# Packing the odd chunk's gate and up rows into one product, moving attention ticks and down products at quarter ends, and shifting weight splits, start tiles and the last steps

## The chip, the cores and the metric

The kernel runs on one core of a Trainium2 chip. The metric is the time of one execution in microseconds of device time; the number to beat is the median of three runs of the kernel before. The engines are named as the profile names them: PE (TensorE matmuls), PEld (its weight loads), DVE (VectorE), ACT (ScalarE), POOL (GpSimd) and SP (SyncE, which only issues DMAs here).

## The reference

`x` is 16 x 64 tokens of width 256, so 1024 tokens. Two layers follow each other, each an attention to a context of 64 keys per batch row and then a feed-forward part, each added to `x` with a gate `tanh(g)`.

```python
x = x + tanh(g_xattn[0]) * L0_xattn(layernorm(x), ctx, ctx)      # 32 query heads, 8 key heads, 64 keys
x = x + tanh(g_ffn[0])   * L0_ffn(layernorm(x), ...)             # hidden size 704, weights int32
x = x + tanh(g_xattn[1]) * L1_xattn(layernorm(x), ctx, ctx, Wc, bc)   # 16 heads in 4 groups, then Wc and bc
x = x + tanh(g_ffn[1])   * L1_ffn(layernorm(x), ...)             # 32 experts of 96, the best 8 per token

# L0_ffn: W = (wq - 128) * scale[:, None]
gate = silu(einsum('bsd,hd->bsh', x, Wgate)); up = einsum('bsd,hd->bsh', x, Wup)
return einsum('bsh,dh->bsd', gate * up, Wdown)

# L1_ffn: masked_w holds a softmax over the 8 largest router logits of a token, zero for the other experts
g = einsum('th,eih->tei', x, w_gate_proj); u = einsum('th,eih->tei', x, w_up_proj)
h = silu(g) * u * masked_w[:, :, None]
return einsum('tei,ehi->th', h, w_down_proj)
```

## The kernel before

**Tiles and passes.** The 1024 tokens are eight tiles of 128 (TT). The hidden rows of both feed-forward parts are cut into chunks of 128: the dense one has 704 rows, which is five full chunks and one of 64 padded with zeros to 128 (F0 = 6), the experts have 24 (MC). A loop of 72 steps `s` runs over passes: passes 0 to 3 are the dense part, each a quarter of the tokens (256) and six steps; passes 4 and 5 are the experts, each half of the tokens (512) and 24 steps. All experts are computed for all tokens, and the routing weights mask them.

**Precision.** A large product is three matmuls into one bank: high part by high part, low part of the data by high part of the weights, and high by low (`product`; L1298, L1299, L1300). So weights and hidden values are split into a high part (ACT: `wh`, `hh`) and the low remainder (`wl`, `hl`). The remainder of the dense weights is made by DVE (`w_low`, L948) from the integers, that of the experts by POOL (L558). SP loads weights into three buffers (`load`, L469) and waits with the fourth load until the first buffer has been split. Behind that load stand in SP's program the DMAs that move key blocks (`move_keys`, L461).

**One step.** PE computes gate(s) into bank 0, up(s) into bank 1, and down(s-1) into banks 2 to 5. Between them ACT makes `tanh` of the gate, DVE makes `(1 + tanh) * gate` (`gate`, L999) and its product with the up bank (`multiply`, L1009 in the dense part, L1012 for the experts); for the experts DVE then multiplies by the routing weights, which PE has spread over the partitions in bank 7 (`weigh`, L1018). ACT rounds the result to `hh`, and DVE takes the rest `hl` (`split_h`, L1023). So down(s) can only run a step later.

**Attention beside it.** An attention block is a tick: scores of the next block (L1156), values of an earlier one (L1195) and transposes of the present one's probabilities (L1176), with maximum, difference, reciprocal and normalising on DVE (L891, L899, L909, L916), the exponential on ACT (L705). The first sixteen ticks of layer 0 run alone, ahead of step 0. All further ones are put into steps by the table `BESIDE`: for a step, a list of ticks at place 0 (between gate and up) and a list at place 1 (behind down). `tick(k, n)` of the same place stands on each engine in that engine's own step, so the table orders all queues at once.

**Ends of quarters.** When a quarter is through, ACT scales the result (`take_out`), PE transposes it back into bank 2 (`back_quarter`) in step 7, 13, 19 or 25 (`BACK_AT`), and DVE adds it to `x` (`add_quarter`, L1034). The first down product of the next quarter writes the same bank and waits for that.

```python
if s in BACK_AT:
    back_quarter(BACK_AT[s])
for k, n in beside(s, 0):
    tick(k, n)
up(s)
if s:
    down(s - 1)
for k, n in beside(s, 1):
    tick(k, n)
if s + 1 in START:
    q_transposes(A[1], START[s + 1] * HT)
```

**Start of layer 1.** Its attention runs in two halves, which `START` opens at steps 14 and 27: layer norm of the first tiles, `q_split` on POOL (L537, L540), `q_transposes` (L1134), `scores`.

**End.** After step 71 the last down product runs, ACT and DVE scale the two banks, PE transposes eight blocks (L1368), DVE adds them to `x` tile by tile (L1040), SP stores.

## Time and profile before

| | us |
|---|---|
| three runs | 422.61, 424.72, 425.23 |
| median | 424.72 |
| the profiled execution's own time | 426.17 |
| its span in the profile | 424.3 |
| mean granted TensorE clock, as a share of full speed | 0.988 |

The profiled execution has 1.87 us outside its span and lies 1.45 us above the median. Sixteen ticks alone fill the time up to about 50 us, the dense quarters with attention beside them the next 130 or so, and from then on the experts' steps, the second half of layer 1's attention beside the first of them. "PEclk" is the clock that was granted to TensorE, as a share of full speed: 1.0 is 2.4 GHz, 0.5 is 1.2 GHz. A wait is put down to the instruction whose end released it.

### The profile page before, as it was taken

The page shows a single profiled execution, that of the slowest core. Times are in us where ns is not written, and L with a number is a line of the kernel's source. Part 1 is how long each engine was busy: PE and PEld are TensorE (multiplying, and loading weights), DVE is VectorE, ACT ScalarE, POOL GpSimd, SP SyncE. Part 2 cuts the span into 40 slices and gives each one's busy share as a digit, 9 for nine tenths or more (in the row PEclk, how much of TensorE's full clock was granted, in tenths as well). Part 3 has the DMA queues.
Part 4 walks back from the last instruction along what each step waited for, and adds up shares of the span by engine and source line. Part 5 has one row for each costly group of instructions (what it writes and reads, how often), then busy time and mean ns, then how long its engine had stood idle before and what let it go on. Part 6 is the DMA issues. An engine that isn't in the chain of part 4 may idle for free.

```text
span 424.3 us, 6897 instructions
## 1 busy us (share of the span) xinstructions
PE 387.4 (91%) x2258; PEld 336.1 (79%) x2258; DVE 302.2 (71%) x612; ACT 220.7 (52%) x441; POOL 174.2 (41%) x201
## 2 busy tenths in 40 slices
PE   4888989989977987969999999999999999999994
PEld 3777879979967977958788778888787888888883
DVE  5699888777755777677777676665877666666664
ACT  3577866556455653545655544445444444444431
POOL 5954332512435113247534343554353444353510
PEclk9999899989998999999999999999999999999999
DMA  5911211110000110032221211223223243323101
GB/s 132 274 45 49 50 28 31 50 44 0 2 0 10 21 20 3 4 110 76 75 76 54 72 50 63 76 74 108 70 85 100 86 133 104 103 84 111 39 0 49
DMA packets 20818, 27.16 MB, mean 64 GB/s; under 512 B 10928, under 2 KB 13616, under 8 KB 20784
## 3 DMA queue, kind: packets, MB, share of 16 engines
q1 hardware_dynamic: 20784, 26.73, 21.7%
q8 instruction: 18, 0.29, 0.3%
q14 instruction: 16, 0.13, 0.1%
HBM read 24.36 MB, written 1.05 MB: 60 GB/s over the span
## 4 chain that ended last, share of the span: by engine, by line
PE 48%; DVE 4%; ACT 1%; SPq 1%; issue 1%; DMA 1%; POOL 0%; DVEq 0%; ACTq 0%
PE bank L1298 14%; PE bank L1300 14%; PE bank L1299 14%; PE bank L1195 1%; SPq L461 1%; PE bank L1218 1%; PE bank L1176 1%; PE bank L1156 1%; PE bank L1385 1%; DMA kbd<-khl 1%; DVE t_t L1012 0%; DVE h_t L1018 0%; DVE t_t L999 0%; DVE hl L1023 0%; POOL wl L558 0%
## 5 line engine op out<-in xcount | busy, mean ns | idle before, releaser
L558 POOL TENSOR_TENSOR wl<-wraw,wh 128x768 fp32r<-128x768 f32 x48 | 88.8, 1850 | 105.1 <-DVE hl L1023 105.1
L1298 PE MATMUL bank<-xh,wh 128*128 128x512 f32 (+1 forms) x288 | 108.5, 377 | 2.8 <-DVE t_t L999 2.7
L1300 PE MATMUL bank<-xh,wl 128*128 128x512 f32 (+1 forms) x288 | 102.5, 356 | 0.0
L1299 PE MATMUL bank<-xl,wh 128*128 128x512 f32 (+1 forms) x288 | 102.3, 355 | 0.0
L656 ACT ACTIVATE hh<-h_t 128x512 fp32r<-128x512 f32 (+1 forms) x72 | 40.3, 560 | 98.7 <-DVE h_t L1018 81.2
L1298 PEld LDWEIGHTS bank<-xh,wh 128*128 128x128 f32 x288 | 54.9, 191 | 10.7 <-DVE t_t L999 2.2
L1023 DVE TENSOR_TENSOR hl<-h_t,hh 128x512 fp32r<-128x512 f32 (+1 forms) x72 | 43.4, 603 | 24.8 <-ACT hh L656 24.7
L1300 PEld LDWEIGHTS bank<-xh,wl 128*128 128x128 f32 x288 | 54.6, 190 | 7.9
L1299 PEld LDWEIGHTS bank<-xl,wh 128*128 128x128 f32 x288 | 55.0, 191 | 6.7
L999 DVE SCALAR_TENSOR_TENSOR t_t<-s_t,bank 128x512 f32<-128x512 f32 (+1 forms) x72 | 42.9, 595 | 23.6 <-ACT s_t L791 23.0
L1298 PE MATMUL bank<-hh,wh 128*128 128x512 f32 (+1 forms) x144 | 51.6, 359 | 8.7 <-DVE x L1034 5.3
L1195 PEld LDWEIGHTS bank<-vbd,pts 128*128 128x128 f32 x384 | 50.0, 194 | 2.7
L1300 PE MATMUL bank<-hh,wl 128*128 128x512 f32 (+1 forms) x144 | 51.2, 356 | 0.0
L1299 PE MATMUL bank<-hl,wh 128*128 128x512 f32 (+1 forms) x144 | 51.2, 355 | 0.0
L891 DVE TENSOR_REDUCE mx<-bank 128x8 f32<-128x512 f32 x48 | 33.0, 687 | 24.2 <-PE bank L1156 24.1
L1195 PE MATMUL bank<-vbd,pts 128*128 128x72 f32 x384 | 49.2, 272 | 0.0
L656 ACT ACTIVATE pts<-bank 128x256 f32<-128x256 f32 x96 | 31.5, 381 | 30.5 <-PE bank L1176 30.3
L791 ACT ACTIVATE s_t<-bank 128x512 f32<-128x512 f32 x48 | 28.6, 596 | 26.6 <-PE bank L1300 26.4
L705 ACT ACTIVATE pt<-dt_ 128x512 f32<-128x512 f32 x48 | 30.3, 632 | 20.5 <-DVE dt_ L899 20.4
L656 ACT ACTIVATE wh<-wraw 128x768 fp32r<-128x768 f32 x48 | 40.2, 838 | 0.0
L1156 PE MATMUL bank<-kbd,qt 128*128 128x512 f32 (+1 forms) x128 | 36.0, 386 | 3.1 <-DVE dt_ L899 1.5
L1298 PEld LDWEIGHTS bank<-hh,wh 128*128 128x128 f32 x144 | 27.1, 188 | 14.1 <-issue 5.8
(106 smaller groups left out, 571.9 us busy)
## 6 DMA issues: line engine op xcount, KB each, us to landing
wraw<-w SPq DMA_DIRECT2D x54, 384.0 KB, 3.1
kbd<-khl SPq DMA_DIRECT2D x80, 8.0 KB
out<-x SPq DMA_DIRECT2D x8, 128.0 KB, 2.5
kbd<-khl SPq DMA_DIRECT2D x40, 16.0 KB
x<-x_in SPq DMA_DIRECT2D x2, 256.0 KB, 3.7
ctx_v<-ctx_in SPq DMA_DIRECT2D x2, 256.0 KB, 6.2
x<-x_in SPq DMA_DIRECT2D x1, 512.0 KB, 5.6
ot<-sel_in SPq DMA_DIRECT2D x1, 512.0 KB, 5.2
```

What stands on the lines that cost most here:

```text
L558: ops.tensor_tensor(wl[:, slot, :], wraw[:, i % WRAW, :], wh[:, slot, :].bitcast(F32), ALU.subtract).then_inc(F.w_split, 1)
L656: return nc.scalar.activation(dst, src, ACT.Copy, scale=scale)
L705: nc.scalar.activation(pt[:, n % 2, :], dt_[:, n % 2, :], ACT.Exp, scale=a.scale).then_inc(a.p_ready, 1)
L791: nc.scalar.activation(s_t[:, s % 2, 0:w], bank[GB][:, 0:w], ACT.Tanh, scale=sgh[:, c:c + 1] if s < MOE0 else 0.5).then_inc(F.s_ready, 1)
L891: return chains[a.layer].mark(ops.reduce_max(mx[:, n % 2, :], s, AX.X))
L999: ops.scalar_tensor_tensor(t_t[:, k, 0:w], s_t[:, k, 0:w], 1.0, bank[GB][:, 0:w], ALU.add, ALU.mult).then_inc(F.sg_done, 1)
L1023: ops.tensor_tensor(hl[:, k, 0:w], h_t[:, k, 0:w], hh[:, k, 0:w].bitcast(F32), ALU.subtract).then_inc(F.h_split, 1)
L1156: done = nc.tensor.matmul(bank[a.s_bank(n)][:, i * a.ns:(i + 1) * a.ns], qt[:, t % 2, b2, 2 * gp:2 * gp + 2, :].rearrange("p g s -> p (g s)"),
L1195: done = nc.tensor.matmul(bank[a.v_bank(q)][:, gp * P:gp * P + VW], pts[:, n % 2, j, :], a.values_of(pair, q), start=(pair == 0), stop=(pa ...
L1298: nc.tensor.matmul(o, wh[:, slot, w_sl], rh, start=first, stop=False, skip_group_check=reopened)
L1299: nc.tensor.matmul(o, wh[:, slot, w_sl], rl, start=False, stop=False, skip_group_check=reopened)
L1300: return nc.tensor.matmul(o, wl[:, slot, w_sl], rh, start=False, stop=stop, skip_group_check=reopened)
```

## The change

It has seven parts.

1. **One product for the last chunk.** The sixth dense chunk has 64 real rows. The host now puts its up rows into the 64 padded rows of the gate weights, so that one product of 128 rows gives both: gate in partitions 0 to 63 of bank 1, up in 64 to 127. In steps 5, 11, 17 and 23 (`halved`) PE computes no gate(s); the joint product stands where up(s) stands. `tanh` and `(1 + tanh) * gate` read bank 1, `multiply` reads its upper half.
2. **Quarter ends.** In steps 7, 13 and 19 the ticks of place 0 go to place 1, and in all steps of `BACK_AT` down(s-1) comes behind the ticks of place 1.
3. **Splitting the dense weights.** ACT first writes the integers as floats (`w_float`, into the new tile `wf`), then copies these to `wh`; POOL instead of DVE makes `wl`. A buffer is free for the next load once `wf` is made.
4. **Start of layer 1.** Layer norm of the second start tile, its `q_split`, the q copies and `q_transposes` come one step earlier; on POOL the second `q_split` now stands ahead of the next `power`.
5. **Experts.** `weigh` is applied to `(1 + tanh) * gate` ahead of the up product's arrival, `multiply` makes the result; the matmul that spreads the routing weights stands ahead of up(s).
6. **The end.** The sums up to step 69 are taken out at step 70 (unscaled); in step 71 eight fp32 matmuls with the identity put them, tokens as rows, into banks 2 and 3 (`open_rows`). The down products of steps 70 and 71 then take the hidden values as the stationary side and add rows on top (`down_rows`), and two DVE instructions scale and add `x`, followed by the stores (`add_pair`). The scaled take-out, the eight transposes and the four additions behind step 71 are gone.
7. `x_high` of layer 1 waits for the gate product's count, since the halved steps have no up count.

```diff
-          12: (((0, 31),), ((0, 32),)), 13: (((0, 33),), ((0, 34),)), 14: (((1, 0),), ((0, 35),)),
+          12: (((0, 31),), ((0, 32),)), 13: ((), ((0, 33), (0, 34))), 14: (((1, 0),), ((0, 35),)),
...
+def halved(s):
+
+    return s < MOE0 and s % F0 == F0 - 1
...
+def gate_bank(s):
+    return UB if halved(s) else GB
...
-                    sp.wait_ge(F.w_split, i - WRAW + 1)
+                    sp.wait_ge(F.wf_ready if i - WRAW < F0 else F.w_split, i - WRAW + 1)
...
-                slot = (i - F0) % SLOTS
-                ops.tensor_tensor(wl[:, slot, :], wraw[:, i % WRAW, :], wh[:, slot, :].bitcast(F32), ALU.subtract
+                slot = (i if i < F0 else i - F0) % SLOTS
+                src = wf[:, i % 2, :] if i < F0 else wraw[:, i % WRAW, :]
+                ops.tensor_tensor(wl[:, slot, :], src, wh[:, slot, :].bitcast(F32), ALU.subtract
...
+                if s + 2 in START:
+                    q_split(A[1], START[s + 2] * HT + 1)
                 if s + 1 in START:
                     t = START[s + 1] * HT
                     power(A[1], t + 2, t + 4)
-                    q_split(A[1], t + 1)
...
+            def w_float(i):
+                act.wait_ge(F.w_loaded[i % WRAW], 16 * (i // WRAW + 1))
+                if i >= 2:
+                    act.wait_ge(F.w_split, i - 1)
+                nc.scalar.activation(wf[:, i % 2, :], wrawi[:, i % WRAW, :], ACT.Copy, bias=-ZERO_POINT
+                                     ).then_inc(F.wf_ready, 1)
...
                 if i < F0:
-                    nc.scalar.activation(wh[:, i, :], wrawi[:, i % WRAW, :], ACT.Copy, bias=-ZERO_POINT
-                                         ).then_inc(F.wh_ready, 1)
+                    act.wait_ge(F.wf_ready, i + 1)
+                    copy(wh[:, i, :], wf[:, i % 2, :]).then_inc(F.wh_ready, 1)
...
+                if 2 <= n < 2 + 3 * F0 and (n - 2) % 3 == 0:
+                    w_float((n - 2) // 3)
...
-                if s + 1 in START:
-                    layer_norm(A[1], START[s + 1] * HT + 1)
-                    q_copy(A[1], START[s + 1] * HT)
-            take_out(2 + QP - 1)
+                if s + 2 in START:
+                    layer_norm(A[1], START[s + 2] * HT + 1)
+                    q_copy(A[1], START[s + 2] * HT)
...
+            def weigh(s):
+                k = s % 2
+                dve.wait_ge(F.sg_done, s + 1)
+                dve.wait_ge(R.spread_done, (pass_of(s) - QP) * QUADS + quad(s) + 1)
+                ops.tensor_tensor(t_t[:, k, :], bank[MASK][:], t_t[:, k, :], ALU.mult).then_inc(F.weighed, 1)
...
+                if halved(s):
+                    ops.scalar_tensor_tensor(h_t[0:HALF, k, 0:w], bank[UB][HALF:P, 0:w], suh[0:HALF, c:c + 1],
+                                             t_t[0:HALF, k, 0:w], ALU.mult, ALU.mult).then_inc(F.m_done, 1)
...
+                    dve.wait_ge(F.weighed, s - MOE0 + 1)
+                    ops.tensor_tensor(h_t[:, k, :], bank[UB][:], t_t[:, k, :], ALU.mult).then_inc(F.m_done, 1)
...
+                dve.wait_ge(F.pair_done, i + 1)
+                ops.scalar_tensor_tensor(x[:, t0:t0 + 2, :], bank[BACK[1][2 * i]][:].rearrange("p (t d) -> p t d", d=DM),
+                                         tg[:, 3:4], x[:, t0:t0 + 2, :], ALU.mult, ALU.add).then_inc(F.x_done, 2)
...
-                multiply(s)
                 if s >= MOE0:
                     weigh(s)
+                multiply(s)
...
             split_h(STEPS - 1)
-            take_out(QP + 1)
-            for t in range(HT):
-                add_tile(QP + 1, t)
+            for i in range(HT // 2):
+                add_pair(i)
...
             def gate(s):
+                if halved(s):
+                    return
...
+                projection(s, GB, 0).then_inc(F.g_done, 1)
+
+            def projection(s, b, at):
+                tok = tokens(pass_of(s))
                 for h in range(KC):
-                    done = product(bank[GB][:, 0:width(s)], slice(h * P, (h + 1) * P), slot_of(s), xh[:, h, tok],
+                    done = product(bank[b][:, 0:width(s)], slice(at + h * P, at + (h + 1) * P), slot_of(s), xh[:, h, tok],
...
+                if halved(s):
+                    if s < F0:
+                        pe.wait_ge(F.w_split, s + 1)
+                    projection(s, UB, 0).then_inc(F.g_done, 1)
+                else:
+                    projection(s, UB, DM).then_inc(F.u_done, 1)
...
+            def open_rows():
+
+                pe.wait_ge(F.ot_act, KC * QP + 2)
+                pe.wait_ge(F.ot_dve, 2)
+                pe.wait_ge(F.x_done, TT + HT)
+                for t in range(HT):
+                    for h in range(KC):
+                        nc.tensor.matmul(bank[BACK[1][t]][:, t % 2 * DM + h * P:t % 2 * DM + (h + 1) * P],
+                                         ot[:, h, t * P:(t + 1) * P], ident[:], start=(t % 2 == 0 and h == 0), stop=False,
+                                         skip_group_check=True)
+
+            def down_row(s, t, hs, ws):
+                return nc.tensor.matmul(bank[BACK[1][t]][:, t % 2 * DM:(t % 2 + 1) * DM], hs[:, s % 2, t * P:(t + 1) * P],
+                                        ws[:, slot_of(s), 2 * DM:3 * DM], start=False, stop=last(s), skip_group_check=True)
+
+            def down_rows(s):
+
+                pe.wait_ge(F.hh_ready, s + 1)
+                for t in range(HT):
+                    down_row(s, t, hh, wh)
+                    down_row(s, t, hh, wl)
+                pe.wait_ge(F.h_split, s + 1)
+                for t in range(HT):
+                    done = down_row(s, t, hl, wh)
+                    if last(s) and t % 2:
+                        done.then_inc(F.pair_done, 1)
+                if not last(s):
+                    done.then_inc(F.dn_done, 1)
...
+                if s == STEPS - 1:
+                    open_rows()
                 for k, n in beside(s, 0):
                     tick(k, n)
+                if s > MOE0 and (s - MOE0) % CPQ == 0:
+                    spread(s)
                 up(s)
-                if s:
-                    down(s - 1)
+                if s == MOE0:
+                    spread(s)
+                if s and s not in BACK_AT:
+                    down_rows(s - 1) if by_rows(s - 1) else down(s - 1)
                 for k, n in beside(s, 1):
                     tick(k, n)
-                if s + 1 in START:
-                    q_transposes(A[1], START[s + 1] * HT)
-            down(STEPS - 1)
-            for t in range(HT):
-                back_tile(QP + 1, t)
+                if s in BACK_AT:
+                    down(s - 1)
+                if s + 2 in START:
+                    q_transposes(A[1], START[s + 2] * HT)
+            down_rows(STEPS - 1)
...
-    down0 = np.pad(A(L0_ffn_wq_down).T, ((0, pad), (0, 0)))
+    down0 = np.pad(A(L0_ffn_wq_down).T, ((0, pad), (0, 0)), constant_values=int(ZERO_POINT))
+    gate0[HIDDEN:] = up0[HIDDEN - HALF:HIDDEN]
```

The next rows are PE's in step 7, the end of the first quarter: bank0 is gate, bank1 up, bank2 holds the quarter's transposed result and the next quarter's down product, bank3 and bank4 scores, bank5 transposed probabilities, bank6 values. Before:

```order
L1300 MATMUL bank0<-xh,wl 128x256
L1358 MATMUL bank2<-ident,ot 128x128 x4
L1233 MATMUL bank7<-ident,xm 128x128 x2
L1156 MATMUL bank4<-kbd,qt 128x512 x2
L1195 MATMUL bank6<-vbd0,pts 128x72 x4
L1176 MATMUL bank5<-ident,pt 128x128 x4
L1298 MATMUL bank1<-xh,wh 128x256
...
L1298 MATMUL bank2<-hh,wh 128x256
```

And after:

```order
L1405 MATMUL bank2<-ident,ot 128x128 x4
L1342 MATMUL bank1<-xh,wh 128x256
...
L1277 MATMUL bank7<-ident,xm 128x128 x2
L1200 MATMUL bank4<-kbd,qt 128x512 x2
L1239 MATMUL bank6<-vbd0,pts 128x72 x4
L1220 MATMUL bank5<-ident,pt 128x128 x4
L1342 MATMUL bank2<-hh,wh 128x256
```

The tick's rows (L1233 to L1176 before) have moved from ahead of the up product to between it and the down product that follows the transposed result in bank 2.

DVE in the same step: `x` is the quarter's addition, `t_t` and `h_t` are gate and multiply of step 7, the rows from `mx` to `gws` are the tick's. Before:

```order
L891 TENSOR_REDUCE mx<-bank4 128x8
L909 RECIPROCAL rc<-bank6 128x16
L916 TENSOR_TENSOR yt<-bank6,rc 64x2x8x8 x2
L942 TENSOR_TENSOR xl<-bank7,xh 128x2x128
L899 TENSOR_TENSOR dt_<-bank4,mx 128x512
L973 CAST gws<-gw 128x2x32
L975 TENSOR_TENSOR gws<-gw,gws 128x2x32
L1034 TENSOR_TENSOR x<-bank2,x 128x512
L999 SCALAR_TENSOR_TENSOR t_t<-s_t,bank0 128x256
L1009 SCALAR_TENSOR_TENSOR h_t<-bank1,suh,t_t 128x256
```

And after:

```order
L1070 TENSOR_TENSOR x<-bank2,x 128x512
L1027 SCALAR_TENSOR_TENSOR t_t<-s_t,bank0 128x256
L1047 SCALAR_TENSOR_TENSOR h_t<-bank1,suh,t_t 128x256
L927 TENSOR_REDUCE mx<-bank4 128x8
L945 RECIPROCAL rc<-bank6 128x16
```

The addition, gate and multiply now stand ahead of the whole tick.

POOL around step 12, where layer 1 starts: `qs` are the two halves of a split query tile, `x<-x,yt` is a residual addition of layer 0, `ve`, `rstd`, `nmr` belong to layer norms. Before:

```order
L540 TENSOR_TENSOR qs<-xn,qs 128x4x64
L575 TENSOR_TENSOR x<-x,yt 128x256
L523 TENSOR_SCALAR ve2<-mv2 128x1
L525 TENSOR_TENSOR rstd2<-ve2,neghalf 128x1
L527 TENSOR_SCALAR nmr2<-mv2,rstd2 128x1
L507 TENSOR_SCALAR ve<-mv 128x2
L510 TENSOR_TENSOR rstd<-ve,neghalf 128x2
L514 TENSOR_SCALAR nmr<-mv,rstd 128x1 x2
L537 TENSOR_TENSOR qs<-xn,one 128x4x64
L540 TENSOR_TENSOR qs<-xn,qs 128x4x64
```

And after:

```order
L565 TENSOR_TENSOR qs<-xn,qs 128x4x64
L562 TENSOR_TENSOR qs<-xn,one 128x4x64
L565 TENSOR_TENSOR qs<-xn,qs 128x4x64
L601 TENSOR_TENSOR x<-x,yt 128x256
L548 TENSOR_SCALAR ve2<-mv2 128x1
```

The second start tile's split no longer stands behind the residual addition and the two groups of layer-norm rows.

## Rows read from the trace of the kernel before

**Rows 1.** PE's waits: us in total, times, longest.

```profile
PE bank L1298 <- DVE x L1034: 5.3, 3, 2.0
```

**Rows 2.** Windows: length; PE, PEld, DVE, ACT, POOL busy; PEclk, DMA share, GB/s.

```profile
21.00:50.00 29.00, 25.92 (x181) 23.22 (x180) 26.96 (x57) 22.75 (x54) 12.81 (x22) 0.94 0.14 38
93.50:94.80 1.30, 1.30 (x8) 1.30 (x7) 0.97 (x5) 0.21 (x1) 0.00 (x0) 0.50 0.00 0
322.00:413.00 91.00, 91.00 (x404) 74.98 (x403) 61.20 (x91) 40.44 (x62) 37.09 (x21) 1.00 0.28 84
```

**Rows 3.** Groups by form, weight splits: count | busy, mean ns | idle before, releaser.

```profile
L948 DVE SCALAR_TENSOR_TENSOR wl<-wraw,wh 128x768 fp32r<-128x768 int32 x6 | 6.3, 1058 | 0.1
L734 ACT ACTIVATE wh<-wraw 128x768 fp32r<-128x768 int32 x6 | 5.0, 836 | 0.0
L558 POOL TENSOR_TENSOR wl<-wraw,wh 128x768 fp32r<-128x768 f32 x48 | 88.8, 1850 | 105.1 <-DVE hl L1023 105.1
```

**Rows 4.** SP's queue, its wait for the first split: us, times, longest.

```profile
SPq L469 <- DVE wl L948: 9.1, 1, 9.1
```

**Rows 5.** Timeline of the opening, POOL and SP's queue: start, us, instruction.

```profile
21.44 1.28 POOL L567 TENSOR_TENSOR khl<-ctx_k,khl 128x512 fp32r<-128x512 f32 x1
25.07 11.71 SPq L461 DMA_DIRECT2D kbd<-khl  x16
```

**Rows 6.** Timeline of PE, steps 7 and 8; idle time and releaser in brackets.

```profile
87.71 0.38 PE L1233 MATMUL bank<-ident,xm 128*128 128x128 f32 x2
...
89.59 0.36 PE L1298 MATMUL bank<-xh,wh 128*128 128x256 f32 x1
...
92.49 0.36 PE L1298 MATMUL bank<-hh,wh 128*128 128x256 f32 x1 [1.94 <-DVE x L1034]
...
93.52 0.41 PE L1298 MATMUL bank<-xh,wh 128*128 128x256 f32 x1
...
97.65 0.36 PE L1298 MATMUL bank<-xh,wh 128*128 128x256 f32 x1
97.85 0.28 PE L1299 MATMUL bank<-xl,wh 128*128 128x256 f32 x1
97.97 0.28 PE L1300 MATMUL bank<-xh,wl 128*128 128x256 f32 x1
```

**Rows 7.** Timeline of DVE, step 7: the quarter's addition.

```profile
91.66 0.68 DVE L1034 TENSOR_TENSOR x<-bank,x 128x512 f32<-128x512 f32 x1
```

**Rows 8.** Timeline of PE, steps 12 to 14, and step 19.

```profile
118.94 0.38 PE L1298 MATMUL bank<-xh,wh 128*128 128x256 f32 x1 [0.82 <-DVE t_t L999]
...
130.43 1.10 PE L1134 MATMUL bank<-ident,qs 128*128 128x128 f32 x4 [2.89 <-POOL qs L540]
...
132.89 0.56 PE L1298 MATMUL bank<-xh,wh 128*128 128x256 f32 x1
...
168.59 0.35 PE L1298 MATMUL bank<-hh,wh 128*128 128x256 f32 x1 [1.99 <-DVE x L1034]
```

**Rows 9.** Timeline of POOL and DVE, steps 12 to 14.

```profile
118.85 0.74 POOL L540 TENSOR_TENSOR qs<-xn,qs 128x256 fp32r<-128x256 f32 x1
...
127.58 0.69 DVE L891 TENSOR_REDUCE mx<-bank 128x8 f32<-128x512 f32 x1 [0.48 <-PE bank L1156]
```

**Rows 10.** The groups by form: layer 1's projection (columns as in rows 3).

```profile
L1218 PE MATMUL bank<-wc,yts 128*128 128x256 f32 x32 | 8.4, 386 | 0.0
```

**Rows 11.** Timeline of the end, all engines.

```profile
413.97 0.39 PE L1300 MATMUL bank<-xh,wl 128*128 128x512 f32 x1
...
417.32 0.50 PE L1298 MATMUL bank<-hh,wh 128*128 128x512 f32 x1 [1.60 <-DVE hl L1023]
...
419.88 1.06 PE L1368 MATMUL bank<-ident,ot 128*128 128x128 f32 x8 [0.89 <-ACT ot L656]
420.32 1.42 DVE L1040 TENSOR_TENSOR x<-bank,x 128x256 f32<-128x256 f32 x4 [0.55 <-PE bank L1368]
```

83 lines of the change are left out of this document (40 added, 43 removed), and 4 rows, old and new, of the table BESIDE.

## The prediction

> **What bounds the kernel now.** Start with PE's share of the span, which is above nine tenths: a change pays here only if it takes work from PE or takes away a wait of PE, or raises the clock at which PE works. The windows [rows 2] then split the kernel by stages. From 322 to 413 us the experts run with PE busy for all of 91.00 us at a granted clock of 1.00, while DVE has 61.20 and POOL 37.09: in this stage reordering DVE's work gains nothing, and I cost the new order of weigh, multiply and the spreading matmul at nothing. The cover is PE's own queue, and DVE's 29.8 us of slack in 91; a loss would need this slack to be used up. From 21 to 50 us, where the ticks run alone, PE has 25.92 of 29.00, but DVE 26.96, and POOL only 12.81: DVE is the fullest engine there. Next come PE's waits [rows 1]: the longest kind is the down product that waits for the quarter's addition to x, 5.3 us in three places, and these lie in the dense quarters between 87 and 169 us. Last, the timelines of the steps named show what each wait costs besides its own length: after the one of 1.94 us [rows 6] the clock was granted at half for a while (0.50 from 93.50 to 94.80, the lower of the two levels, 1.2 GHz [rows 2]).
>
> All terms are differences within the profiled execution. It took 1.45 us more than the median, an effect I take to be the same for both kernels, so the sum is subtracted from the median, 424.72.
>
> **Opening: gain 1.8 us.** Six DVE instructions of 1058 ns leave DVE, 6.3 us [rows 3]; most of them lie in the window in which DVE has 26.96 of 29. ACT gets six more, which I price like its other conversions of the same tile, 836 ns [rows 3]: 5.0 us on 22.75, of which some 3.4 fall in the window, so about 26.1 of 29. POOL gets six at 1850 ns [rows 3], 11.1 us; with 12.81 of 29 it has room, but a result that comes 0.8 us later. PE's own waiting in the window is 29.00 - 25.92 = 3.1 us, which no relief of DVE can exceed. There is a second bound: SP waited 9.1 us for the first weight split [rows 4], and behind that wait the key blocks were moved, starting at 25.07 [rows 5]. Their source was finished at 21.44 + 1.28 = 22.72 [rows 5]. If the load waits for the float copy only, the moves start at most 2.35 us earlier; their 11.71 us of issuing are the same. So the gain lies between 2.9 (the smaller relief, plus a little after the moves) and a loss of 1.0, if ACT, which now carries 26.1, delays the exponentials by one conversion. I take 1.8, nearer to the upper end, since DVE is the engine that is full and ACT stays below what DVE has now.
>
> **Packed products: gain 0.6 us.** Four gate products of six matmuls go. At full clock one matmul of this form follows the next after 0.12 us (97.85 to 97.97 [rows 6]), so 24 x 0.12 = 2.9 us of PE work is the upper end. But gate of the next step now waits for tanh and the DVE instruction behind it, which can only begin after the joint product, and that product stands where up stood. Before, this chain ran under the up product. What is left on PE beside it is the down product (six matmuls, 0.7 us), and the tick at place 0 has moved ahead. The chain is one instruction of ACT and one of DVE on 256 columns, about 0.4 us each as an estimate from the 0.68 us of DVE on 512 [rows 7], plus hand-overs, and ACT and DVE may still be in their tick. So each of the four places gives 0.7 at best and zero at worst; two of them (steps 17 and 23) lie where attention of layer 1 keeps DVE busy. I take a fifth of the upper end, 0.6; the lower end is zero.
>
> **Step 7: gain 3.4 us.** Now: quarter transposes, the tick's PE work from 87.71 to 89.59 (1.88 us), up, then a wait of 1.94 us, down at 92.49 [rows 6]. The wait exists because DVE comes to the addition only at 91.66 [rows 7], after the whole tick, although its source was transposed before 87.71 [rows 6]. With addition, gate and multiply ahead of the tick on DVE, and the tick's 1.88 us of PE work between up and down, the addition has long ended when down is reached: the 1.94 us go. The work in between is the same, so down would start at 90.55. The six matmuls of down took 1.03 us (92.49 to 93.52), at full clock 0.72: 0.3 more. Then gate(8) and its tick took 93.52 to 97.65, 4.13 us [rows 6], much of it at the lower clock; gate at 0.72 and a tick like that of step 7 with four query transposes, 2.2 as an estimate, make 2.9, so 1.2 more if the clock stays up because PE no longer stands still. 1.94 + 0.3 + 1.2 = 3.4. The lower end is a third, if the moved tick waits for its own inputs: its transposed probabilities come from DVE's difference, which now stands later. The DVE work ahead of it is the addition, gate and multiply, which begin at about 88 instead of 91.66, so I think the tick's DVE rows slip by about 1.5 us and still end before PE needs them in step 8.
>
> **Steps 12 to 14: gain 2.7 us.** Two waits go: the quarter's (5.3 - 1.94 - 1.99 = 1.4 us [rows 1, 6, 8]) and the 2.89 us for the second query split of layer 1 on POOL at 130.43 [rows 8], since POOL now does it behind the first. Two come. The first query transposes, now at the end of step 12, wait until 118.85 + 0.74 = 119.59 [rows 9]; PE was free at 118.94 - 0.82 = 118.12 [rows 8], so 1.5 us, of which 0.82 was lost already. Behind them wait gate(13) and all of step 13. And the first scores of layer 1 now have nothing between them and their own exponential: DVE's maximum, at 127.58 now [rows 9], comes about 0.7 earlier (DVE has the addition, gate and two moved ticks before it), and then maximum, difference and exponential at 0.69 each (two at the row's length, the third taken alike) end near 129.0. Transposes and the remaining PE work of the tick put up(14) at about 130.2 instead of 132.89 [rows 8]: 2.7. Bounds: 0.7 lost if neither wait really goes, 4.3 if both go and no new one comes.
>
> **Step 19: gain 0.4 us.** The wait of 1.99 us [rows 8] goes as in step 7, but the two moved ticks of layer 1 contain transposes and router logits that wait for DVE's low parts in the same step, so most of it should return under another name. Bounds 0 and 2.0.
>
> **The end: gain 0.6 us.** The last down product began at 417.32, waiting for hl [rows 11]. With hidden values stationary, its eight matmuls on hh run while DVE makes hl; only four remain: 0.5 us, to 417.8. Two additions of twice the width, 0.75 each as an estimate (the four narrow ones took 1.42 together), end at 419.3. Now the additions end at 420.32 + 1.42 = 421.74 [rows 11], so 2.4 us go. Against that, the opening of the row sums puts eight fp32 products ahead of the last up product, where PE is the bound. The nearest row is the projection: 32 passes of 256 columns for 16 matmuls in 8.4 us [rows 10], 0.26 each. At 128 columns 16 passes cost 0.105 to 0.13 each, 1.7 to 2.1 us; I take 1.8. 2.4 - 1.8 = 0.6, with bounds 0.3 and 0.7.
>
> The sum is 1.8 + 0.6 + 3.4 + 2.7 + 0.4 + 0.6 = 9.5, and 424.72 - 9.5 = 415.2 us.
>
> **Rivals.** (a) *The stalls get new names.* The ticks moved behind up wait for their own chains, and quarter ends give a third: 1.1 instead of 3.4 and 0.9 instead of 2.7, so 4.1 less: 419.3. For it speaks that a tick's PE work is a chain through DVE and ACT; against it that the chain of step 7 has nearly all its inputs from step 6. (b) *Better than forecast.* The packed products give their full 2.9 (2.3 more), the opening 2.9 (1.1 more), and the lower clock behind 130.43, where four query transposes took 1.10 us [rows 8], goes too (about 1.2): 410.6. (c) *POOL's splits hold the opening back.* The weight split takes 1850 ns on POOL and 1058 on DVE [rows 3], and if each of the six stands on the path of loads and ticks, the opening is 6 x 0.79 = 4.7 us longer instead of 1.8 shorter: 421.7. Against it: POOL has 12.81 of 29 us of work [rows 2], and the first reader of a split is step 0, at about 50 us. The Trainium skill has this rule (GPSIMD Engine Reference, 4.1 Engine selection): two-input elementwise work belongs on VectorE, GpSimd being about half as fast; the rows agree on the ratio (1.75), and by that rule (c) would be the outcome. (d) *Slower than before.* All of the conversions come onto the path: ACT's six at 0.836 stand ahead of the tick's other work, and POOL's six at 1.85 stand ahead of the key parts and layer-norm rows that the next tiles need. Each exposed pair costs 2.69 us, six cost 16.1, against 7.7 of all other gains: 433.1. It decides from 2.9 exposed pairs on; POOL's idle half and SP's earlier release speak against it. That the change does not do what it says I exclude for the order of rows, which shows every move.
>
> **How the numbers follow.** Forecast 0.55, (a) 0.20, (b) 0.12, (c) 0.09, (d) 0.04. The forecast's own bounds are about 412 to 418.5. The range takes in most of (a) and (b) and reaches towards (c): 409.5 to 420.5. One per cent, 4.25 us, is about what a measurement of this kernel can tell from no change. Faster than 420.5 are the forecast, (b) and nearly all of (a): 0.85; (c) is within 1%: 0.10; slower 0.05.
>
> **What would show it.** Right: PE's wait for the quarter's addition is nearly gone from its waits; down(6) follows its tick without a gap and the clock around step 8 stays at 1.00; POOL's wl rows lie in the opening, and step 0 begins about 2 us earlier; no wait of the query transposes of 2.9 us; the end from the last up product about 2.4 us shorter and the row opening of 1.8 us before it. Wrong: waits of the same length on transposes of probabilities or on scores in steps 7, 13 and 19; key moves that start no earlier than 25 us; ACT full up to 50 us; gate products of steps 6, 12, 18 and 24 that wait a microsecond for DVE.

## The result, and the profile after

| | us |
|---|---|
| before, four runs | median 424.93 (422.61 to 425.23) |
| changed, four runs | median 417.86 (415.61 to 418.55) |
| ratio, 95% interval | 0.984 (0.981 to 0.987) |
| profiled execution, changed | 417.80, span 415.7, mean granted clock 0.982 |

The change takes 7.1 us off; 9.5 were forecast, and 417.86 lies within the range. Six more runs of the same kernel gave 418.27 (ratio 0.982, 0.979 to 0.985). One of the four executions of mid_19 below was disturbed (2112.1 us), and its median is that of the other three.

Where the time went is read from a landmark that both traces have once in each step: the start of DVE's `hl` row, behind which the step's down product can run. The table gives the start in both profiles; the last column is what the stretch between two rows of the table gained. What follows step 71's landmark is in the last line.

| step | before | after | difference | gained in between |
|---|---|---|---|---|
| 0 | 58.09 | 54.27 | -3.82 | 3.8 |
| 6 | 86.92 | 83.31 | -3.61 | -0.2 |
| 8 | 102.18 | 94.65 | -7.53 | 3.9 |
| 12 | 119.96 | 112.28 | -7.68 | 0.15 |
| 16 | 149.64 | 139.35 | -10.29 | 2.6 |
| 18 | 163.44 | 153.15 | -10.29 | 0 |
| 20 | 174.74 | 167.11 | -7.63 | **-2.7** |
| 30 | 222.82 | 215.68 | -7.14 | -0.5 |
| 70 | 412.49 | 404.32 | -8.17 | 1.0 |
| end of the span | 424.3 | 415.7 | -8.6 | 0.4 |

So four stretches gained, as forecast, and one lost clearly. The spans differ by 8.6 us and the medians by 7.1, since the profiled execution of before, 426.17 us, lies 1.24 above its median. The 0.5 us lost from step 20 to 30 are a stretch of the lower clock (0.50 from 176 to 178 us): without one, these steps took 48.08 us before and 47.73 in after_2. The waits of PE in the changed kernel (answer to [rows 1]; us in total, times, longest):

```profile
PE bank L1200 <- DVE dt_ L935: 4.3, 3, 2.6
...
PE bank L1294 <- DVE xl L978: 2.3, 2, 2.1
...
PE bank L1178 <- POOL qs L565: 1.7, 1, 1.7
```

The wait for the quarter's addition (5.3 us) is gone. In its place stand waits for `dt_` (the second scores of layer 1 wait for DVE's difference of the first; 1.5 us before) and for `xl` (router logits wait for DVE's low part; 0.2 us before).

Step 7, PE, the rows that answer to [rows 6]:

```profile
83.82 0.36 PE L1342 MATMUL bank<-xh,wh 128*128 128x256 f32 x1
...
84.61 0.38 PE L1277 MATMUL bank<-ident,xm 128*128 128x128 f32 x2
...
86.50 0.36 PE L1342 MATMUL bank<-hh,wh 128*128 128x256 f32 x1
...
87.29 0.28 PE L1342 MATMUL bank<-xh,wh 128*128 128x256 f32 x1
...
90.12 0.36 PE L1342 MATMUL bank<-xh,wh 128*128 128x256 f32 x1
```

Up, the tick, and down follow each other without a gap: from up to down 2.68 us, where it was 2.90 with the wait in it and the tick outside. Gate(8) and its tick take 87.29 to 90.12, 2.83 us instead of 4.13. DVE adds the quarter ahead of the tick (answer to [rows 7]):

```profile
84.17 0.69 DVE L1070 TENSOR_TENSOR x<-bank,x 128x512 f32<-128x512 f32 x1 [0.44 <-PE bank L1405]
```

Steps 12 to 14 and 19 on PE (answer to [rows 8]):

```profile
111.96 0.66 PE L1178 MATMUL bank<-ident,qs 128*128 128x128 f32 x4 [1.66 <-POOL qs L565]
...
120.58 1.09 PE L1200 MATMUL bank<-kbd,qt 128*128 128x256 f32 x4 [2.65 <-DVE dt_ L935]
...
158.31 0.42 PE L1294 MATMUL bank<-gws,xh 128*128 128x64 f32 x1 [2.06 <-DVE xl L978]
...
159.53 0.56 PE L1342 MATMUL bank<-hh,wh 128*128 128x256 f32 x1
```

The waits for the first query split (1.66 us, 1.5 was forecast) and of layer 1's second scores for its first are the two that the forecast named. In step 19 the wait of 1.99 us became one of 2.06 us, for another row of DVE. What it cost besides stands in the windows (columns as in [rows 2]; PEclk is the number ahead of the last two):

```profile
21.00:50.00 29.00, 25.73 (x192) 22.80 (x191) 23.74 (x55) 26.10 (x60) 19.86 (x30) 1.00 0.15 40
88.00:92.00 4.00, 4.00 (x34) 3.87 (x33) 3.86 (x13) 2.47 (x6) 0.89 (x3) 1.00 0.06 23
...
158.50:166.00 7.50, 7.50 (x35) 7.03 (x36) 2.66 (x10) 1.73 (x4) 1.91 (x5) 0.56 0.01 2
322.00:405.00 83.00, 83.00 (x367) 68.18 (x366) 56.09 (x83) 37.37 (x59) 34.07 (x19) 1.00 0.27 83
```

Behind the wait of step 19 PE worked at 0.56 for 7.5 us, mostly at the lower level of 1.2 GHz; before, the same steps ran at 1.00:

```profile
168.00:176.00 8.00, 7.10 (x55) 6.78 (x56) 5.61 (x17) 3.69 (x9) 2.35 (x6) 1.00 0.01 2
```

The wait of 2.65 us in step 14 was followed by the lower clock too:

```profile
121.00:124.00 3.00, 3.00 (x16) 3.00 (x15) 1.88 (x4) 2.39 (x6) 2.27 (x4) 0.50 0.06 14
```

In the opening ACT has the forecast 26.10 us, and DVE is down from 26.96 to 23.74. The splits and the key moves (answers to [rows 3 to 5]):

```profile
L584 POOL TENSOR_TENSOR wl<-wf,wh 128x768 fp32r<-128x768 f32 x6 | 11.0, 1829 | 0.7 <-ACT wh L685 0.7
```

```profile
SPq L494 <- ACT wf L764: 2.7, 1, 2.7
```

```profile
22.71 11.71 SPq L486 DMA_DIRECT2D kbd<-khl  x16
```

SP waits 2.7 us instead of 9.1, and the key moves start at 22.71, within 0.01 of the bound worked out (22.72); what they wait for now is their own source (`khl` on POOL, 3.8 us). In all ten profiles with the early release they start between 22.55 and 22.79. The end (answer to [rows 11]):

```profile
404.83 2.05 PE L1426 MATMUL bank<-ident,ot 128*128 128x128 f32 x16
...
407.87 0.40 PE L1344 MATMUL bank<-xh,wl 128*128 128x512 f32 x1
...
410.77 0.64 PE L1431 MATMUL bank<-wh,hl 128*128 128x256 f32 x4
411.30 1.41 DVE L1082 SCALAR_TENSOR_TENSOR x<-bank,tg,x 128x512 f32<-128x512 f32 x2 [0.91 <-PE bank L1431]
```

Opening the rows takes 1.8 us of PE (404.83 to 406.64, where up begins), as priced. From the last up matmul to the end of the additions it is 4.84 us (407.87 to 412.71) instead of 7.77 (413.97 to 421.74).

### The profile page after: what moved, and what is told of

Its sections match the earlier page's. It is cut to its first block, busy times and chain, and to the rows that moved or that the text cites. A ratio compares the mean times of both kernels' runs of the same rounds, so it can differ in the third digit from the quotient of the medians.

```text
span 415.7 us, 6902 instructions
## 1 busy us (share of the span) xinstructions
PE 382.7 (92%) x2254; PEld 332.5 (80%) x2254; DVE 297.2 (72%) x604; ACT 223.2 (54%) x447; POOL 183.5 (44%) x207
## 4 chain that ended last, share of the span: by engine, by line
PE 53%; DVE 3%; issue 1%; ACT 1%; DVEq 0%; ACTq 0%
PE bank L1342 15%; PE bank L1344 15%; PE bank L1343 15%; PE bank L1239 1%; PE bank L1220 1%; PE bank L1262 1%; PE bank L1200 1%; PE bank L1461 1%; PE bank L1431 1%; DVE t_t L1034 1%; DVE h_t L1051 1%; DVE t_t L1027 1%; PE bank L1426 0%; PE bank L1451 0%; DVE rep L1098 0%
## 5 line engine op out<-in xcount | busy, mean ns | idle before, releaser
L1342 PE MATMUL bank<-xh,wh 128*128 128x512 f32 (+1 forms) x280 | 106.7, 381 | 2.5 <-DVE t_t L1027 2.3
L1344 PE MATMUL bank<-xh,wl 128*128 128x512 f32 (+1 forms) x280 | 101.0, 361 | 0.0
L1343 PE MATMUL bank<-xl,wh 128*128 128x512 f32 (+1 forms) x280 | 100.9, 360 | 0.0
L1343 PEld LDWEIGHTS bank<-xl,wh 128*128 128x128 f32 x280 | 53.9, 193 | 6.9
L1342 PE MATMUL bank<-hh,wh 128*128 128x512 f32 (+1 forms) x140 | 50.3, 359 | 1.9 <-DVE hl L1056 1.8
L1239 PEld LDWEIGHTS bank<-vbd,pts 128*128 128x128 f32 x384 | 48.9, 191 | 2.6
L1344 PE MATMUL bank<-hh,wl 128*128 128x512 f32 (+1 forms) x140 | 49.8, 356 | 0.0
L1343 PE MATMUL bank<-hl,wh 128*128 128x512 f32 (+1 forms) x140 | 49.7, 355 | 0.0
L1200 PE MATMUL bank<-kbd,qt 128*128 128x512 f32 (+1 forms) x128 | 33.5, 365 | 5.7 <-DVE dt_ L935 4.3
L1051 DVE TENSOR_TENSOR h_t<-bank,t_t 128x512 f32<-128x512 f32 x48 | 33.2, 692 | 6.3 <-PE bank L1344 1.4
```

The costliest lines, as they stand in the source:

```text
L1051: ops.tensor_tensor(h_t[:, k, :], bank[UB][:], t_t[:, k, :], ALU.mult).then_inc(F.m_done, 1)
L1200: done = nc.tensor.matmul(bank[a.s_bank(n)][:, i * a.ns:(i + 1) * a.ns], qt[:, t % 2, b2, 2 * gp:2 * gp + 2, :].rearrange("p g s -> p (g s)"),
L1239: done = nc.tensor.matmul(bank[a.v_bank(q)][:, gp * P:gp * P + VW], pts[:, n % 2, j, :], a.values_of(pair, q), start=(pair == 0), stop=(pa ...
L1342: nc.tensor.matmul(o, wh[:, slot, w_sl], rh, start=first, stop=False, skip_group_check=reopened)
L1343: nc.tensor.matmul(o, wh[:, slot, w_sl], rl, start=False, stop=False, skip_group_check=reopened)
L1344: return nc.tensor.matmul(o, wl[:, slot, w_sl], rh, start=False, stop=stop, skip_group_check=reopened)
```

## The experiments

Two questions were open: what each part is worth by itself, and why step 19 lost. Each kernel is the changed one with one part undone, if nothing else is said. "Local" is read from the same landmark, against the changed kernel's profile. The kernels ran in different comparisons, in which the kernel before had medians from 424.44 to 425.37 us, so the ratio tells more than the median. Only u_split and mid_14 differ from the changed kernel by more than the intervals, u_load just; the others are read at the landmarks alone.

| kernel | median us | ratio to before (95%) | local difference |
|---|---|---|---|
| u_split | 419.84 | 0.989 (0.988 to 0.990) | opening +4.4 |
| u_load | 421.25 | 0.990 (0.987 to 0.993) | opening +3.3 |
| u_half | 416.21 | 0.979 (0.976 to 0.982) | steps 5 to 17 +0.5 |
| u_quarters | 418.26 | 0.984 (0.982 to 0.987) | steps 7, 8 +2.2; 13 to 15 +0.8; 19, 20 -1.3 |
| u_start | 418.56 | 0.984 (0.980 to 0.988) | steps 14, 15 +2.2 |
| u_19 | 417.11 | 0.983 (0.980 to 0.986) | step 19 +0.8; step 20 -1.9 |
| mid_19 | 415.84 | 0.979 (0.975 to 0.983) | step 20 -3.3 |
| u_weigh | 419.24 | 0.984 (0.980 to 0.987) | steps 30 to 70 +0.1; end +0.7 |
| u_tail | 416.50 | 0.982 (0.977 to 0.987) | end +0.5 |
| after_2 | 418.27 | 0.982 (0.979 to 0.985) | steps 12 to 14 +1.6 |
| mid_14 | 413.24 | 0.971 (0.968 to 0.975) | step 13 +1.6; steps 14 to 16 -2.1; step 20 -3.3 |

**u_19: step 19 in its old order.**

```diff
-19: ((), ((1, 9), (1, 10)))
+19: (((1, 9),), ((1, 10),))
...
-                if s and s not in BACK_AT:
+                if s and (s not in BACK_AT or s == 19):
...
-                if s in BACK_AT:
+                if s in BACK_AT and s != 19:
                     down(s - 1)
```

> The changed kernel with step 19 alone as before (first tick between gate and up, second behind the down product). First theory: in the changed kernel the wait of 2.0 us in step 19 only moved to the router logits, and the low clock behind it (0.50 from 159 to 165 us) cost what step 7 and steps 12 to 14 had won beyond; with the old order the wait for the quarter's addition is back at 2.0 us, the clock stays up behind it as it did before, and steps 19 and 20 take some 2.7 us less: about 415.2 us. Rival: the clock falls there for the work of the steps ahead of it, whatever waits: low clock stays, about 417.9 us.

The old wait is back at its old length, PE's timeline:

```profile
159.02 0.36 PE L1342 MATMUL bank<-hh,wh 128*128 128x256 f32 x1 [1.98 <-DVE x L1070]
```

```profile
159.00:167.00 8.00, 7.67 (x47) 7.18 (x48) 4.36 (x14) 2.81 (x7) 1.88 (x5) 0.79 0.01 2
```

The clock fell here too, to 0.79 over these 8 us, half of what the changed kernel lost in its window. So neither theory holds as put: the old order does not keep the clock up. Nor does the new one make it fall each time: u_start, which has the new order of step 19 and the same wait of 2.1 us, went through it at full clock:

```profile
158.00:166.00 8.00, 5.63 (x43) 5.13 (x43) 5.08 (x17) 1.95 (x5) 2.80 (x7) 1.00 0.01 2
```

From the landmark of step 18 to that of step 20, at full clock, the old order took 11.30 us (both profiles of before) and the new one 11.34 (u_start). With 1.7 us of clock lost they took 12.88 (u_19) and 12.87 (after_2), and with 3.4 lost the changed kernel's profile took 13.96. At the same clock the order gives nothing. The clock fell there in seven of eight profiles with the new order and in two of four with the old one, too few to say whether the order makes the fall likelier.

**mid_19: the down product between the two ticks.**

```diff
-                for k, n in beside(s, 1):
+                for j, (k, n) in enumerate(beside(s, 1)):
                     tick(k, n)
-                if s in BACK_AT:
+                    if s in (19,) and j == 0:
+                        down(s - 1)
+                if s in BACK_AT and s not in (19,):
                     down(s - 1)
```

> The changed kernel with the down product of step 19 between its two ticks instead of behind both. First theory: its 0.7 us of matmuls fill a third of the wait of 2.06 us for the low part that the router logits read; if the clock then stays up, some 3 us less, about 415 us. Rival: only the wait gets shorter and the clock still falls to a half behind it: 0.7 us less, about 417.2 us.

The matmuls fill 0.7 us of the wait, and in the profiled execution the clock stayed at 1.00:

```profile
158.33 0.30 PE L1294 MATMUL bank<-gws,xh 128*128 128x64 f32 x1 [1.30 <-DVE xl L978]
```

```profile
159.00:167.00 8.00, 7.68 (x61) 7.33 (x60) 4.50 (x13) 4.71 (x11) 2.71 (x6) 1.00 0.01 2
```

The step gains 3.3 us there, the first theory's number: 0.7 of wait (10.66 us from step 18 to 20, against 11.34 in u_start), and the rest goes with the clock. Two other executions took 415.84 and 417.26, with mean clocks of 0.985 and 0.986 (0.996 in the profiled one). So they lost more clock; whether they lost it here is not on record.

**u_quarters: all three quarter ends in the old order.**

```diff
-7: ((), ((0, 25),)), 13: ((), ((0, 33), (0, 34))), 19: ((), ((1, 9), (1, 10)))
+7: (((0, 25),), ()), 13: (((0, 33),), ((0, 34),)), 19: (((1, 9),), ((1, 10),))
...
-                if s and s not in BACK_AT:
+                if s:
...
-                if s in BACK_AT:
-                    down(s - 1)
```

> The changed kernel with the ticks of steps 7, 13 and 19 and the down products at quarter ends as before. First theory: the order gave 4.0 us at step 7 and about 1.4 at step 13, and took 2.7 at step 19: about 420.6 us, with waits for the quarter's addition of 5 us in three places. Rival: the start of layer 1 one step earlier fills the wait of step 13 anyway: about 419.2 us.

The waits for the addition are back, 5.3 us in three places, that of step 13 with them, so the rival's reason falls:

```profile
121.45 0.35 PE L1342 MATMUL bank<-hh,wh 128*128 128x256 f32 x1 [1.37 <-DVE x L1070]
```

Step 7 loses 2.2 us, not 4.0: its wait of 1.94 was not followed by the lower clock in this execution. Step 13 loses 0.8, not 1.4, and step 19 gives back 1.3, not 2.7. The profile is 2.5 us behind at the end, the median 0.4: where the clock falls differs by as much as the part is worth.

**u_split: the dense split as before**, on ACT and DVE, loads released by it. POOL's part and the float copy go, and on DVE:

```diff
+                if n >= 4 and (n - 4) % 3 == 0 and (n - 4) // 3 < F0:
+                    w_low((n - 4) // 3)
```

> The changed kernel with the dense weights split as before: no float copy on ACT, the low part on DVE, loads released by the split. First theory: this part gave all that step 0 came earlier, 3.8 us, so about 421.5 us, and step 0 begins again at about 52.7 us by ACT's first tanh. Rival: half of it came from elsewhere (state of the clock in the opening, 0.94 before and 1.00 after): about 419.7 us.

The median of 419.84 is the rival's number, the trace is the first theory's: the granted clock of the opening is 1.00, ACT's first `tanh` comes at 53.63 us, and step 6 comes 4.4 us later than in the changed kernel. Of this, 1.8 us are made up by step 30, where the changed kernel's profile lost more clock. With the old split the changed kernel reaches step 6 at 87.69 us, the second profile of before (before_2, below) at 87.90; so the other parts give next to nothing up to there.

**u_load: only the release of the loads goes back.**

```diff
-                    sp.wait_ge(F.wf_ready if i - WRAW < F0 else F.w_split, i - WRAW + 1)
+                    sp.wait_ge(F.w_split, i - WRAW + 1)
```

> The changed kernel, in which only the release of the first six loads goes back from the float copy to the finished split (on POOL). Theory: the opening is ahead because the key blocks move earlier, which needs the early release; with it undone SP waits some 9 us again, the moves begin at about 25 us or later, and step 0 comes some 2 to 4 us later: 420 to 422 us. Rival: DVE's relief by the low parts does it alone, and the moves have slack: about 417.9 us, step 0 as early as in the changed kernel.

Undoing all of part 3 costs 4.4 us up to step 6, undoing the release alone 3.3. With the release undone the ticks run as early as in the changed kernel (DVE's twelfth maximum at 35.71 against 35.62; between 39.30 and 40.29 in the three profiles with the old split), and then PE stands still for the keys, which start moving at 26.25:

```profile
39.18 0.73 PE L1200 MATMUL bank<-kbd,qt 128*128 128x512 f32 x2 [2.62 <-DMA kbd<-khl]
```

So DVE's relief makes the first twelve ticks faster, and is given back if the keys don't come earlier too: what is left of it is 1.1 us against u_split, no more than two executions of one kernel differ by in the opening (below). The release without the relief was not tried, since DVE's split reads the buffer that would be released.

**u_half: gate and up of the last chunk apart.**

```diff
-    return s < MOE0 and s % F0 == F0 - 1
+    return False
```

> The changed kernel with six full chunks: gate and up of the last chunk apart, as before (padded gate rows now hold up rows, whose results are multiplied by zero). Theory: the four packed products gave next to nothing, since the gate product of the following step waits for DVE by what was saved: steps 5 to 6, 11 to 12 and 17 to 18 take within 0.2 us the same, 417.7 to 418.4 us. Rival: what was saved is hidden in later waits, and taking it back costs the full 2.9 us: 420.8 us.

Steps 6 to 8 lose 0.4 us, steps 10 and 11 another 0.2, step 17 nothing: the theory's end, not the rival's 2.9. Small as it is, it stands clear at the landmarks: from step 5 to step 8 u_half takes 16.71 us, ten other profiles with the packed product and the new order 16.34 to 16.36. In the total it doesn't show, the median of u_half is 1.65 us below that of the changed kernel.

**u_start: the start of layer 1 as before,** on PE, and likewise on ACT and POOL:

```diff
-                if s + 2 in START:
-                    q_transposes(A[1], START[s + 2] * HT)
+                if s + 1 in START:
+                    q_transposes(A[1], START[s + 1] * HT)
```

> The changed kernel with the start of layer 1 as before (layer norm, query split, copies and transposes of the second start tile in the step ahead of the start). Theory: this part gave most of the 2.6 us of steps 12 to 14, the wait of 2.9 us for the query split is back and those of 1.7 and 2.6 us go: 1 to 1.5 us more, about 419 us. Rival: the quarter's order of step 13 gave them: within 0.3 us of 417.9.

The wait for the query split is back, and longer than it was before:

```profile
122.47 1.11 PE L1177 MATMUL bank<-ident,qs 128*128 128x128 f32 x4 [4.35 <-POOL qs L565]
```

The part is worth 2.2 us at its place, the larger share of the 2.6, and more than the 1 to 1.5 of the theory. At the second start of layer 1 (step 27) it is worth another 0.3: from step 20 to 30 u_start took 48.03 us and after_2 47.73, both at full clock.

**u_tail: the end as before.** On PE:

```diff
-                if s == STEPS - 1:
-                    open_rows()
...
-            down_rows(STEPS - 1)
+            down(STEPS - 1)
+            for t in range(HT):
+                back_tile(QP + 1, t)
```

> The changed kernel with the end as before (down products with weights as the stationary side to the last, take-out, eight transposes, four additions). Theory: the row sums save 2.4 us behind the last up product and cost some 2.0 ahead of it: 0.4 us more, 418.3 us, the span from the last tanh of ACT to the end back at 11.3 us from 10.8. Rival: the opening of the rows is paid by the clock or hidden, and 2.4 us come back: 420.3 us.

Landmark 71 comes 1.3 us earlier without the row opening, and the span ends 0.5 us later, both beside the lead of 1.7 us that this execution had gained in the steps ahead: the theory's size.

**u_weigh: the experts' order as before.** On DVE (with the operands of both instructions, and the spreading matmul behind up):

```diff
+                multiply(s)
                 if s >= MOE0:
                     weigh(s)
-                multiply(s)
```

> The changed kernel with the order of the experts' steps as before: multiply by the up product first, routing weights after, the spreading matmul behind up. Theory of the prediction: PE bounds these steps, no difference there: steps 30 to 70 as long as in the changed kernel within 0.2 us. Rival: between steps 30 and 60 the changed kernel gained 1.0 us on the one before, and this order is what gave it: steps 30 to 70 take 1 us longer.

Steps 30 to 70 are 0.1 us longer: the order gave nothing there, as forecast, and the rival falls. Only the landmark of step 71 comes another 0.7 us later, the length of one DVE instruction, which at the end no product of a next step covers. DVE waits for the last up product either way, with one instruction left behind it in the changed kernel and two in u_weigh:

```profile
408.30 0.69 DVE L1051 TENSOR_TENSOR h_t<-bank,t_t 128x512 f32<-128x512 f32 x1 [1.40 <-PE bank L1344]
```

```profile
409.64 0.69 DVE L1051 TENSOR_TENSOR t_t<-bank,t_t 128x512 f32<-128x512 f32 x1 [2.13 <-PE bank L1344]
```

u_tail and u_weigh together show that the two parts need each other. From the landmark of step 70 to the end of the span it is 11.8 and 11.9 us in the two profiles of before, 11.9 with the new order alone (u_tail), a little over 12.0 with the row sums alone (u_weigh), and 11.4 with both.

**before_2: the kernel before once more.**

> The kernel before, as it is, profiled once more. Open are two differences between the two profiles: some 1.0 us between steps 30 and 54, which none of the parts undone gave back, and a stretch of the lower clock in the opening (41 to 46 us) that the changed kernel did not show there. First theory: both belong to that one execution; here steps 30 to 54 take as long as in the changed kernel within 0.3 us, and the lower clock lies elsewhere. Rival: they belong to the kernel before: steps 30 to 54 are again 1 us longer, and the opening again has the stretch behind the same wait.

It took 424.48 us at a clock of 0.996. From step 30 to step 70 it needed 188.85 us, the changed kernel 188.64, the first profile of before 189.67: 0.8 of the 1.0 us belongs to that one execution (it lies in step 33), and 0.2 may be the change's. The opening shows no lower clock, and step 0 comes 1.0 us later all the same; the key moves began at 26.07. So the lower clock of the opening belongs to the one execution, as the first theory has it, and cost it nothing that shows: the first profile was 0.99 us ahead of this one before the stretch (DVE's twelfth maximum at 39.30 and 40.29) and 0.98 after it, at step 0. Step 7 has the same wait as before, and this time the clock stayed up behind it:

```profile
93.47 0.35 PE L1298 MATMUL bank<-hh,wh 128*128 128x256 f32 x1 [1.94 <-DVE x L1034]
```

```profile
93.00:97.00 4.00, 3.53 (x29) 3.47 (x30) 3.28 (x10) 1.47 (x4) 0.00 (x0) 1.00 0.01 4
```

**after_2 and mid_14.** mid_14 has mid_19's edit, and in step 14 the first tick of layer 1 behind up and down:

```diff
-14: (((1, 0),), ((0, 35),))
+14: ((), ((1, 0), (0, 35)))
```

> The changed kernel as it is, once more, beside the next two on the same chip. Theory: its executions differ by how many stretches of the lower clock they hold (two in the opening profile of before, four in its own), so the times spread over some 3 us while the mean granted clock goes from 0.98 to 0.99: 415.5 to 418.5 us. Rival: the spread has nothing to do with the clock: executions of the same mean clock differ as much as those of different ones.

> The changed kernel with the down product of step 19 between its ticks, and in step 14 the first tick of layer 1 behind up and down products instead of between gate and up. Theory: the 1.4 us of matmuls fill more than half of the wait of 2.6 us that the second scores have for DVE's difference, and fewer stretches of the lower clock follow: 1 to 3 us less than the changed kernel, 414 to 416.5 us. Rival: DVE comes to maximum and difference later by gate and multiply, so the wait only moves behind the down product: no gain at step 14, and what is gained comes from step 19.

The six times of after_2 with their clocks: 417.81 (0.984), 416.64 (0.988), 419.97 (0.982), 416.50 (0.985), 418.72 and 418.74 (0.988). The spread of 3.5 us is about the expected one, though three of the six lie above 418.5. Equal clocks differ by 2 us, so the mean clock explains only a part; what makes the rest is not shown. In mid_14 the second scores wait 0.30 us instead of 2.65, the down product 1.04 for `hl`:

```profile
121.84 0.39 PE L1342 MATMUL bank<-hh,wh 128*128 128x256 f32 x1 [1.04 <-DVE hl L1056]
...
125.49 0.71 PE L1200 MATMUL bank<-kbd,qt 128*128 128x256 f32 x4 [0.30 <-DVE dt_ L935]
```

```profile
120.00:126.00 6.00, 4.66 (x35) 3.98 (x33) 5.75 (x14) 2.98 (x8) 4.11 (x10) 1.00 0.02 5
```

So a part of the wait moved to the down product and the rest is gone, and the rival falls: from step 13 to 16 mid_14 took 18.42 us, after_2 20.56, of which 1.7 us of lost clock. In step 13, which both have alike, the lower clock followed the wait for the first query split in both (8.10 us from step 12 to 13, against 6.53 in the changed kernel's profile). mid_14 is the fastest kernel here: 413.24 us against 418.27 in the same comparison, its interval clear of the changed kernel's. Its mean clocks, 0.983 to 0.998, lie mostly above those of after_2, 0.982 to 0.988; how much of the 5.0 us is the waits and how much the clock is not separated.

## Why the prediction was right, and where its terms were not

The mechanisms named were there, but for the term of step 19, which failed, and the zero for the experts' order, which did not hold at the end. That the sum came close is in part luck: the opening gave 1.8 us more than forecast and step 19 took 3.1 more, and 0.8 of the 8.6 us between the spans is a delay of the first profile in step 33 that no part of the change removes.

**Opening, forecast 1.8, read 3.6 to step 6.** The mechanism was right, the key moves above all, to the hundredth of a microsecond; the size was not. Two things were missing. One is the pace of PE in the first 17 us. The first query transposes, in the profile of before and in that of after:

```profile
8.72 1.11 PE L1134 MATMUL bank<-ident,qs 128*128 128x128 f32 x4 [0.69 <-DVE qs L1081]
```

```profile
8.77 0.66 PE L1178 MATMUL bank<-ident,qs 128*128 128x128 f32 x4 [0.67 <-DVE qs L1124]
```

The granted clock is shown as 1.00 from 5 to 17 us in both. The pace differs between executions of one kernel: ten profiles with the changed opening reached step 6 between 82.96 and 84.31, the three with the old split between 86.92 and 87.90. mid_14, which is the same kernel up to step 13 and had the slow pace to about 18 us, as the first profile of before had, was the latest of the ten. Like against like the part is worth 86.92 - 84.31 = 2.6 us; the other 1.0 of the 3.6 is pace. The second is that I took 1.8 between bounds whose upper end, 2.9, was nearer: the moves' 2.35 us came through in full.

**Packed products, forecast 0.6, shown 0.5** by u_half. Gate of the following step waits for DVE, as worked out: 0.53 and 0.98 us at 76.65 and 105.79 in the trace.

**Step 7, forecast 3.4, read 3.9;** 2.2 without the clock (u_quarters, and 2.4 against before_2). The two terms, 2.2 for the wait and 1.2 for the lower clock, are about right in size (2.2 to 2.4 and 1.6), but the second is there only in executions in which the clock falls, one of the three profiled with the old order.

**Steps 12 to 14, forecast 2.7, read 2.6.** Both new waits came where they were named. u_start shows that most of it is the earlier start. Here the clock was on the forecast's side: in after_2 it fell behind the first of the two waits, and steps 12 to 16 took 28.66 us instead of 27.07, only 1.0 less than in the first profile of before.

**Step 19, forecast a gain of 0.4, read a loss of 2.7.** This is the step that failed. The renamed wait was foreseen, with the engine and the row, but it came back whole (2.06 for 1.99 us), so no 0.4 us were left: at full clock the order is worth 11.30 - 11.34, which is nothing. What was not priced is that the lower clock followed the wait in this execution and had not done so in that of before, although step 7 was costed by just this effect. u_19 and u_start show that the clock can fall in the old order and stay up in the new. So the loss is not the order's: 13.96 - 11.34 = 2.6 us of it go with the clock. Why the clock falls in one execution and not in another stays open.

**The end, forecast 0.6, shown 0.5. The experts, forecast 0, shown 0.1** for the reordering up to step 70. The zero was wrong for the last step, where PE's queue no longer covers DVE: there the new order is worth 0.7 us (u_weigh), and without it the row sums gain nothing. So the forecast of the end came out right with a term that it had put at nothing. The part behind the last up product got 2.9 us shorter, not 2.4, the opening of the rows cost 1.8 as priced, and the stretch from the last addition to the end of the span, which the sum left out, is 0.4 longer.

Rival (a), stalls under new names, is what happened in step 19 and in part in step 14, but not in step 7. Of rival (b) the larger opening came, and neither the 2.9 us of the packed products nor the full clock behind the start of layer 1 (0.50 from 121 to 124 us). Rival (c) falls: the split takes 1829 ns on POOL, 1.73 times the 1058 on DVE, and the opening is shorter all the same. The Trainium skill's rule (GPSIMD Engine Reference, 4.1 Engine selection) holds as a ratio and not as a result here, since POOL had the room and DVE had not. Rival (d) falls with it.

## What to carry to other kernels

A relief of one engine shows its worth only if the next limit moves too: ask what stops the stage next, and undo the halves separately to see it. A wait that a reorder removes must be followed to the next row that reads the same engine, and the cheapest fill is the work that already stands behind it: moving one down product and one tick into two waits (mid_14) gave another 5.0 us, 418.27 to 413.24, in part through the clock. A part costed at nothing because another engine covers it is to be looked at again in the last step, where the cover ends. Where single executions differ by as much as a part is worth, read the part at a landmark inside the trace, not from the total, and compare stretches with the same granted clock.

## What was not expected of the hardware

The same wait of 1.94 us in the same program was followed by the lower clock in one execution (before, 0.58 from 93 to 97 us) and by full clock in another (before_2, 1.00, above):

```profile
93.00:97.00 4.00, 4.00 (x22) 3.87 (x20) 1.82 (x7) 1.49 (x3) 0.00 (x0) 0.58 0.02 4
```

Summed over windows of one microsecond as length times one minus PEclk, and without the stretch at the very end, the profiles of these kernels hold between 1.7 us (before_2) and 10.2 us (u_load) of it, mostly at the same few places, but not at each of them in every execution. And PE's pace in the first 17 us differs between executions of one kernel, 1 us at step 6, without a sign of it in the granted clock of the two rows above; in after_2 part of it shows, as 0.66 from 12 to 17 us.
